# A two-layer graph block on one core: W2's product formed as rows of nodes, the second attention joined to the first without a barrier, and the edge counting set up by VectorE alone

## What is computed

```python
# h: 1024 nodes x 768, 16384 edges (src, dst), dst sorted
def gat_layer(x, W, a_s, a_d, b):
    h = (x @ W).reshape(n, H, C)
    alpha_s, alpha_d = einsum('nhc,hc->nh', h, a_s), einsum('nhc,hc->nh', h, a_d)
    e = leaky_relu(alpha_s[src] + alpha_d[dst], 0.2)
    e = exp(e - segment_max(e, dst)[dst])
    alpha = e / (segment_sum(e, dst)[dst] + 1e-16)
    return segment_sum(h[src] * alpha, dst) + b
def gat(x):            # first: 8 heads of 768; second: 1 head of 768
    return gat_layer(elu(gat_layer(x, W1, ..., b1)), W2, ..., b2)
def gcn(x):            # two graph convolutions with self-loops, relu between
    ...
x = layernorm(x + gat(x))
x = layernorm(x + gcn(x))
```

## Time and profile before

| | us |
|---|---|
| median of 3 runs (lowest to highest) | 1761.97 (1761.91 to 1763.41) |
| the profiled execution | 1763.09 |
| its span | 1761.3 |
| PE busy | 1673.9 (95%), 7596 matmuls |
| DVE busy | 1224.3 (70%) |
| ACT busy | 797.5 (45%) |
| POOL busy | 166.4 (9%) |

### The profile page before, as it was taken

How to read it: one execution, slowest core, us unless ns; L and a number is a source line. 1 busy time by engine, 2 the same in 40 slices (tenths; PEclk the granted TensorE clock), 3 DMA queues, 4 the chain that set the end, 5 groups by cost and what they waited for, 6 DMA issues and landing times. The chain is left out here.

```text
span 1761.3 us, 21747 instructions
## 1 busy us (share of the span) xinstructions
PE 1673.9 (95%) x7596; PEld 1393.6 (79%) x7601; DVE 1224.3 (70%) x2336; ACT 797.5 (45%) x1295; POOL 166.4 (9%) x117
## 2 busy tenths in 40 slices
PE   5899999999999999999999899999999976979998
PEld 3588888788877888888888688888888865878898
DVE  8744445644798788778875887788768348974347
ACT  6334322222555556555655565565555325534340
POOL 0022222212200000000000000000000013310003
PEclk9999999999999999999999999999999977989999
DMA  3255564865547476646654665475444231131222
GB/s 136 73 181 193 182 222 160 211 221 167 198 162 185 174 207 164 153 167 205 188 153 151 177 173 127 173 220 146 131 176 176 99 111 48 52 120 55 65 84 103
DMA packets 133808, 268.04 MB, mean 152 GB/s; under 512 B 23738, under 2 KB 83524, under 8 KB 121028
## 3 DMA queue, kind: packets, MB, share of 16 engines
q1 hardware_dynamic: 133700, 266.63, 49.1%
HBM read 206.21 MB, written 60.40 MB: 151 GB/s over the span
## 5 line engine op out<-in xcount | busy, mean ns | idle before, releaser
L41 PE MATMUL bank<-ph,hc 128*128 128x512 f32 x768 | 299.7, 390 | 4.5 <-DVE mean L929 3.3
L43 PE MATMUL bank<-ph,hc 128*128 128x512 f32 x768 | 298.9, 389 | 0.0
L42 PE MATMUL bank<-pl,hc 128*128 128x512 f32 x768 | 298.8, 389 | 0.0
L786 DVE CUSTOM_DVE_ANT_0 junk<-bank,a_bc 128x512 bf16<-128x512 f32 (+1 forms) x256 | 130.0, 555 | 190.1 <-ACT st L532 175.0
L41 PE MATMUL bank<-hh,w2h 128*128 128x512 f32 x576 | 225.7, 392 | 4.5 <-DVE rows L947 4.1
L41 PE MATMUL bank<-wh,xTh 128*128 128x512 f32 x570 | 223.7, 392 | 2.7 <-POOL wl L467 2.7
L43 PE MATMUL bank<-hh,w2l 128*128 128x512 f32 x576 | 225.2, 391 | 0.0
L42 PE MATMUL bank<-hl,w2h 128*128 128x512 f32 x576 | 225.2, 391 | 0.0
L43 PE MATMUL bank<-wh,xTl 128*128 128x512 f32 x570 | 222.5, 390 | 0.0
L42 PE MATMUL bank<-wl,xTh 128*128 128x512 f32 x570 | 222.4, 390 | 0.0
L532 ACT CAST st<-bank 128x512 fp32r<-128x512 f32 x96 | 56.4, 587 | 280.3 <-PE bank L43 249.4
(11 more groups left out here) (257 smaller groups left out, 2877.5 us busy)
## 6 DMA issues: line engine op xcount, KB each, us to landing
hc<-h_scratch SPq DMA_DIRECT2D x96, 1024.0 KB, 5.5
h_scratch<-st SPq DMA_DIRECT2D x96, 512.0 KB, 3.1
w2r<-in_L_gnn_W SPq DMA_DIRECT2D x96, 384.0 KB, 6.7
wr<-in_L_gnn_W SPq DMA_DIRECT2D x12, 1536.0 KB, 8.6
gwr<-in_L_gnn_W SPq DMA_DIRECT2D x24, 384.0 KB, 3.2
row_bc<-logits_scratch SPq DMA_DIRECT2D x16, 512.0 KB, 12.4
expo_bc<-expo_scratch SPq DMA_DIRECT2D x16, 512.0 KB, 6.1
xr<-in_x SPq DMA_DIRECT2D x2, 1536.0 KB, 8.4
```

The source lines that it names most:

```text
L41: nc.tensor.matmul(out, sh, mh, start=first, stop=False, skip_group_check=not grouped)
L42: nc.tensor.matmul(out, sh, ml, start=False, stop=False, skip_group_check=not grouped)
L43: return nc.tensor.matmul(out, sl, mh, start=False, stop=last, skip_group_check=not grouped)
L786: nc.vector.tensor_tensor_reduce(out=junk[:, s % 2, 0:hi - lo], in0=banks[n % 6][:, lo:hi], in1=a_bc[q % 2][:, k, lo:hi], scale=1.0, scala ...
```

## The change

1. `project` swaps its operands: the stationary one is 128 targets of `hh` or `hl`, the moving one all 768 columns of W2. A block's row of 768 lies in one and a half banks (`block_rows`), so it is two matmuls, of 512 and of 256 columns (`pieces`). At u == 8 the rows are copied straight to `rows`, 4 copies by ScalarE; `cols`, the transposes, L947 and its waits are gone.
2. Stage 1 and 2 are one block. In the last unit SP loads the first half's rows and `a2_bc`, VectorE makes their logits, their low parts and the largest logit among those sources (`top_of_early`). Behind the last projection VectorE reads the second half's logits from the banks, TensorE spreads them by a broadcast column times the identity (`spread`), and only the four new source blocks are looked through (`top_of_all`). b2 is added to x by 8 accumulating DMAs that GpSimd issues; GpSimd computes nothing there. ScalarE writes the normalised rows, VectorE all low parts of them.
3. All `hot_low` are made by VectorE, in 16 operations with 16-bit operands; a tile's 128 columns now lie 256 bytes apart. TensorE turns and lessens 8 of the 12 pieces of x before the first window. The registers of a window are loaded in the middle and at the end of the one before.

```diff
-            for j in range(ACT_TILES // TG, ET // TG):
-                nc.vector.tensor_tensor(hot_low[:, j * TG:(j + 1) * TG, :],
-                                        lane[:, 0:P].unsqueeze(1).to_broadcast([P, TG, P]),
-                                        keyT[:, 1, j * TG:(j + 1) * TG].unsqueeze(2).to_broadcast([P, TG, P]), ALU.is_equal).then_inc(low_hot_v, 1)
+            dve.wait_ge(lanes_made, 1)
+            for j in range(ET // TG):
+                nc.vector.tensor_tensor(hot_low[:, 0:P * ET].rearrange("p (l t) -> p l t", t=ET)[:, :, j * TG:(j + 1) * TG], lanes[:, :, :],
+                                        key16[:, j * TG:(j + 1) * TG].unsqueeze(1).to_broadcast([P, P, TG]), ALU.is_equal).then_inc(low_hot, 1)
...
-                for f in range(FB):
-                    fs = slice(f * P, (f + 1) * P)
-                    last = split_products(nc, banks[f][:, :], (w2h[:, g % 3, fs], w2l[:, g % 3, fs]), (hh[:, g % 3, :], hl[:, g % 3, :]),
-                                          u % H == 0 and k == 0, u % H == H - 1 and k == FB - 1, grouped=False)
+                first, final = u % H == 0 and k == 0, u % H == H - 1 and k == FB - 1
+                if first and u:
+                    pe.wait_ge(rows_out, HNB)
+                for c in range(HNB):
+                    bs = slice(c * P, (c + 1) * P)
+                    for lo, hi in pieces(c):
+                        last = split_products(nc, block_rows(c)[:, lo:hi], (hh[:, g % 3, bs], hl[:, g % 3, bs]), (w2h[:, g % 3, lo:hi], w2l[:, g % 3, lo:hi]),
+                                              first and (c % 2 == 0 or lo > 0), final, grouped=False)
+                    if final and c == 1:
+                        last.then_inc(pair_full, 1)
...
-            pe.wait_ge(low_hot_s, ACT_TILES // TG)
-            pe.wait_ge(low_hot_v, (ET - ACT_TILES) // TG)
+            for half in range(2):
+                for g in range(half * XA, half * XA + XA):
+                    turn_x(g)
+                for g in range(half * XA, half * XA + XA):
+                    lessen_x(g)
+            pe.wait_ge(low_hot, ET // TG)
...
-                    mm = nc.tensor.matmul(bank[:, :], hot_low[:, bass.ds(first + j, 1), :].rearrange("p t l -> p (t l)"), hot_key[w % 2][:, j, :],
+                    mm = nc.tensor.matmul(bank[:, :], hot_low[:, bass.ds(first + j, P, ET)], hot_key[w % 2][:, j, :],
                                           start=(j == 0), stop=False, skip_group_check=True)
...
+            dve.wait_ge(pair_full, 2)
+            dve.wait_ge(top2_sum, NB)
+            logit_of(HNB, 0)
+            logit_of(HNB + 1, 0)
+            dve.wait_ge(c_used, U * FB)
+            logit_of(HNB + 2, 0)
+            logit_of(HNB + 3, 0)
+            dve.wait_ge(g_hi, NB - 2)
+            logit_of(HNB, 1)
+            for b in range(HNB):
+                top_of_all(b)
+            exponents2(0)
+            smaller_logits(1)
+            logit_of(HNB + 1, 1)
+            row_low(HNB)
+            row_low(HNB + 1)
+            for half in range(2):
+                for i in range(NB + 1):
+                    if i < NB:
+                        weights2(half, i)
+                    if i >= 1:
+                        weight_low2(half, i - 1)
+                    if (half, i) == (0, 1):
+                        dve.wait_ge(logit2_sum, logits2_by(HNB + 1, 1))
+                        for b in range(HNB, NB):
+                            top_of_all(b)
+                    if (half, i) == (0, 2):
+                        dve.wait_ge(top2_sum, 2 * NB)
+                        logit_of(NB - 2, 1)
+                        logit_of(NB - 1, 1)
+                    if (half, i) == (0, 3):
+                        exponents2(1)
+                    if (half, i) in ((0, 4), (0, 5)):
+                        row_low(NB - 6 + i)
+                    if (half, i) == (1, 0):
+                        for b in range(HNB - 1):
+                            bank_out(b)
+                    if (half, i) == (1, 2):
+                        bank_out(HNB - 1)
...
+            for s in range(NB):
+                pe.wait_ge(p_lo, LATER + s + 1)
+                if s >= NB - 2:
+                    pe.wait_ge(g_lo, s + 1)
+                for c in range(HNB - 1):
+                    last = add_source(0, s, c)
+                    if s == NB - 1:
+                        last.then_inc(agg_full, 1)
+            pe.wait_ge(e_done, LATER + NB)
+            for s in range(NB):
+                last = add_source(0, s, HNB - 1)
+            last.then_inc(agg_full, 1)
```

More of the change, by code:

```diff
@@ L88, in gnn_resnorm @@
         FREE = place[0]
-        banks = [ctx.enter_context(nc.psum_tensor(f"bank{i}", [P, 512], F32)) for i in range(8)]
+        psum = ctx.enter_context(nc.psum_tensor("psum", [P, 8 * 512], F32))
+        banks = [psum[:, 512 * i:512 * (i + 1)] for i in range(8)]
         logits_d = nc.dram_tensor("logits_scratch", [H * NB, P], F32, kind="Internal").ap()
@@ L609, in leave @@
             def leave(i):
-                for f in range(3):
-                    nc.scalar.copy(cols[:, f, :], banks[3 * i + f][:, :]).then_inc(cols_out, 1)
+                for c in range(2):
+                    nc.scalar.copy(rows[i][:, c, :], block_rows(2 * i + c)).then_inc(rows_out, 1)
             def sum_high(v):
@@ L658, in _ @@
                 head_high(g + 2)
+                if not more:
+                    early_high(0)
+                    early_high(1)
                 if u == 0:
@@ L672, in _ @@
                 head_high(g + 3)
+                if not more:
+                    early_high(2)
+                    early_high(3)
                 second_high(g + 4)
@@ L689, in _, with late_high, exponentials2 @@
                     second_high(g + 7)
+            def late_high(c):
+                nc.scalar.copy(gh[1][:, c, 0:D], block_rows(c)).then_inc(g_hi, 1)
+            def exponentials2(half, i):
+                c = LATER + half * NB + i
+                if c >= LATER + 2:
+                    act.wait_ge(p_full, c - 1)
+                for k, (e, bias) in enumerate(((e1b, logit2[:, 0, i:i + 1]), (e2b, logit2_02[:, i:i + 1]))):
+                    if c == LATER:
+                        act.wait_ge(expo2_full, k + 1)
+                    frm = banks[7 - k][:, :] if half == 0 else expo_row[:, k, :]
+                    last = nc.scalar.activation(e[:, i % 2, :], frm, ACT.Exp, bias=bias)
+                last.then_inc(e_done, 1)
@@ L969, in _ @@
                 head_low(g)
+                if not more:
+                    ones_beside()
+                    logit_of(0, 0)
+                    logit_of(1, 0)
                 if more:
@@ L979, in _ @@
                     average(g + 1)
[L980 to L981 removed]
+                if not more:
+                    logit_of(2, 0)
+                    logit_of(3, 0)
                 if more:
@@ L992, in _ @@
                 average(g + 2)
+                if not more:
+                    logit_of(0, 1)
+                    logit_of(1, 1)
                 if more:
@@ L1004, in _ @@
                     sum_rows(v, 3)
-                if u == H:
-                    rows_out(1, range(HNB))
                 if u % H:
                     second_low(g + 3)
+                if not more:
+                    logit_of(2, 1)
+                    logit_of(3, 1)
+                    smaller_logits(0)
                 if more:
@@ L1013, in _ @@
                 average(g + 3)
+                if not more:
+                    row_low(0)
+                    row_low(1)
                 if more:
@@ L1024, in _ @@
                 second_low(g + 4)
+                if not more:
+                    for b in range(HNB):
+                        top_of_early(b)
                 if more:
@@ L1039, in _ @@
                 second_low(g + 5)
+                if not more:
+                    row_low(2)
+                    row_low(3)
                 average(g + 5)
@@ L1244, in _, with spread, add_source @@
                 project(u, 5)
+            def spread(bank, c, column):
+                return nc.tensor.matmul(bank[:, c * P:(c + 1) * P], column.to_broadcast([P, P]), ident[:, :], start=True, stop=True, skip_group_check=True)
+            def add_source(half, s, c):
+                bs = slice(c * P, (c + 1) * P)
+                for i in range(2):
+                    cs = slice(i * HC, (i + 1) * HC + 2 * i)
+                    last = split_products(nc, banks[2 * c + i][:, 0:HC + 2 * i], (p2h[half][:, s, bs], p2l[half][:, s, bs]),
+                                          (gh[s // HNB][:, s % HNB, cs], gl[s // HNB][:, s % HNB, cs]), s == 0, s == NB - 1)
+                return last
@@ new lines, in _ @@
+            pe.wait_ge(a_out, U * FB)
+            for c in range(HNB):
+                pe.wait_ge(logit2_sum, logits2_by(HNB + c, 0))
+                last = spread(banks[6], c, logit2[:, 0, HNB + c:HNB + c + 1])
+            last.then_inc(row_full, 1)
```

(7 more changed lines are left out.)

791 lines of the change are left out of this document (356 added, 435 removed).

## The result

| | before | after |
|---|---|---|
| median (lowest to highest), us | 1761.97 (1761.91 to 1763.41) | 1722.97 (1722.16 to 1723.07) |
| ratio, 95% interval | | 0.9776 [0.9759, 0.9793] |
| the profiled execution, its span | 1763.09, 1761.3 | 1723.07, 1720.9 |

A forecast was written before the change was run, and what follows sets the result against it. TensorE (PE), 95% busy, was taken to bound the kernel, waiting or slow in three places; -11 + 7.7 - 12.2 - 41 = -56.5 against 1763.09 gave 1706.6, median 1706, range 1692 to 1738.

The forecast's parts named there:

- the second attention gives back more: Rival: waits and low clock in the second gather, or a slower tail, give 1718 to 1730 us; chance 0.14.
- D: Second attention, last projection to stage 3: VectorE is the chain, 97.9 us instead of 138.9, -41.
- the narrow step of 0.135: Rival in `project`: 256-column matmuls cost 0.135 us instead of 0.120, total 1723; chance 0.07 for 0.13 to 0.15.
- A: Counting, up to x @ W1: earlier start and shorter windows, x @ W1 at 69 instead of 80.25, -11 us.
- the rival of the columns: Counting: weight loads from `hot_low` columns 256 bytes apart, at 0.44 us, make windows 4.6, total 1738; chance 0.08.
- C: Unit 8: ScalarE's four copies free the banks far ahead of the projection, removing the wait and low clock, -12.2 us.
- such a wait in every block: Sign of being wrong: a wait on ScalarE (`norm_root`, `x1_normed`) ends each block of the tail.
- Pauses of PE between source blocks for some 20 us: Sign expected in the changed profile: TensorE pausing between source blocks of the second gather, some 20 us.
- the others go by VectorE, 2.72 and 0.13 for what is left of the register loads, 2.85: Counting: the eleven windows without a piece of x cost 2.85 us each, after four at 3.5.
- B: Projections: 12 matmuls of 512 and 12 of 256 columns make 4.16 us against 4.08, 96 times, +7.7.
- 0.1735: Projections, upper bound: a 256-column matmul costs what 384 columns do, +69 us; total 1768, slower than before.
- 12 x 0.2266: Projections: the twelve 512-column matmuls of a `project` at 0.2266 us each, read from the kernel before.

The follow-up runs named there:

- ch_early: Changed kernel with six of ScalarE's eight copies of counts moved earlier, into its wait in the second half, and two behind the last `p2h`: 1719.46 us.
- regs_spread: Changed kernel with all register loads of TensorE and VectorE ahead of the counting, between turns of x and one-hots; columns still apart: 1727.82 us.
- packed_regs: Changed kernel with each tile's `hot_low` columns side by side and all register loads ahead of the counting: 1722.42 us.
- apart_read: `packed_regs` with TensorE reading its weights 256 bytes apart from the packed one-hots, so it counts with wrong ones: 1727.05 us.
- wide_first: Changed kernel with all 512-column matmuls of a `project` before all 256-column ones, except in each half's first and last `project`: 1718.51 us.
- sxl_pool: Changed kernel with the low parts of seven blocks' scaled rows made by GpSimd instead of VectorE, from a product ScalarE also writes: 1720.27 us.

## Why the prediction was right or wrong

The time is inside the stated range, but 5 us outside the prediction's own band for its forecast (1696 to 1718, with a chance of 0.60). It lies where the rival "the second attention gives back more" was priced (1718 to 1730), and that rival did not come true: D is only 2.8 us short. Nor did the narrow step of 0.135 that would also give 1723: it is 0.120. A's -2.3 lies outside all the bounds that the prediction worked out for it, -4 to -14, but for the rival of the columns. So it is in part luck that the time fell into the range.

**C was right**: 12.5 us forecast as 12.2.

**D was right in its chain and nearly in size**: -38.3 for -41, VectorE's tail and the 16 us of TensorE's idle time as forecast. Set beside the prediction's own times behind the last projection, the 2.8 us come from three places. The gather starts at 14.45 for 13.2; the fourth target block is through 0.5 later than that explains (50.2 for 48.4); and 1.0 is at the very end, where VectorE stands 2.06 for the last block's `sxh`. The wait of 2.84 for `p2h` was not foreseen, and `ch_early` gives it back, but it is no part of the 2.8: the stretch from the fourth target block to the last low part of the weights took 14.6 with it, where 14.5 had been forecast, so VectorE's own work there was priced as much too high. The pitch of blocks 4 to 7 agrees by coincidence, as the two rows of L1262 and L1325 show. That of blocks 0 to 3 holds a wait of 0.71 for ScalarE; the prediction had named such a wait in every block as a sign of being wrong. "Pauses of PE between source blocks for some 20 us" did not come; the prediction's sum, through at about 40, had no room for them either. The low clock cost little: TensorE was back at the high one with the eleventh matmul of the gather (steps of 0.32, then 0.176).

**A failed**, by 8.9 us (x @ W1 starts at 77.94 for 69), in the step "the others go by VectorE, 2.72 and 0.13 for what is left of the register loads, 2.85". Measured are 3.25 for a steady window. The loads are not hidden by being moved into the window: a pair costs 0.58 us on VectorE (`regs_spread`) and 0.68 a window on TensorE, and taking them out of the packed window makes it 0.71 shorter (`packed_regs`). And VectorE's 2.72, read from the kernel before with its packed weights, does not hold beside weights from columns apart (`apart_read`: 3.00 for 2.63). Only without both is the window VectorE's own (`packed_regs`). Of the 8.9, 5.1 are the eleven windows behind the first four (38.23 to 74.66 for 31.35), 1.0 the first four, 0.7 the later start, and 2.0 an error of counting: 4 + 11 windows are 15, and the sixteenth, 3.28 with its copy (74.66 to 77.94), was in the sum with 1.25.

The rival of the columns apart had the right cause and, for the most part, the wrong effect. A load of 0.21 for 0.097 (not the 0.44 that it took as its end) costs TensorE 0.015 a matmul in the last window (1.86 for 1.74 with eight); the larger effect shows at VectorE. The Trainium skill's rule ("Advanced Engine Details and Errata", "SBUF Cachelines"), that an access on another line each time is slower, agrees with the load of 0.210 against 0.097; no run here shows the size of a line.

**B was right in its step and short in its sum**: 256 columns cost 0.120, as the line through 384 and 512 had it, and 0.1735 is excluded. The missing 4 us are the term "12 x 0.2266": behind narrow matmuls the wide ones take 0.233 on average. `wide_first` takes 3.8 of them back. The "present 59" for a unit was the average of the last eight, with the wait of unit 8 in it; a unit took 57.61 before and takes 58.41 now.

## What to carry to other kernels

A price read from a kernel holds for what ran beside it there: when a change alters how one engine reads memory, look for its cost in the other engines' durations as well. The same holds when a change takes work off an engine: the 2.02 of VectorE's row beside GpSimd is not its price alone (0.68). Before costing a register load at nothing because it was moved, take a pair's price from the pause that the row shows and look for the queue that would cover it. In a tail where two engines hand work to each other, a line moved forward for one stretch gives the wait to the next; work out the pitch of every stretch. And when a forecast pitch comes true, compare the operations in it before calling the mechanism right.

## What the runs showed of the hardware that was not expected

- Weight loads of 128 16-bit columns 256 bytes apart take 0.210 us at the median against 0.097 packed, and raise the median of VectorE's 128x512 operations beside them from 0.344 to 0.420.
- The 128x1024 one-hot operation on 16-bit operands takes 0.61 a step (9.72 for 16) when both operands run along the row, and 1.14 (18.25 for 16) when one stands still in it. The order of the output changes with it, and no run separates the two.
- The six 512-wide matmuls behind six 256-wide ones take 0.233 on average instead of 0.2267.
- In the kernel before, VectorE's write of a 128x768 row takes 2.02 us instead of 0.68 when it starts just behind GpSimd's operation on such a row (`sxl`, 1.85); `bank_out`'s operations and the statistics of a row are not slowed beside it (`sxl_pool`).
